# A two-layer transformer on one core: feed-forward weights prepared inside the first projection

## The chip, the cores and the metric

The kernel runs on one core of a Trainium2 chip. The metric is the device time of one execution in microseconds, as the median of several runs. Times in the profile are microseconds from the start of the profiled execution's span, unless they are marked ns. The engines are PE (matrix multiply, with PEld for its weight loads), VectorE (DVE in the profile), ACT, POOL and SP; SP issues the DMAs.

## The reference, cut to what matters

The sequence has 4096 tokens of 256 features in float32. The first layer is an attention with a low-rank key and value path, then a feed-forward part whose operands are rounded to a 4-bit grid in blocks of 16; the second layer is another attention and another feed-forward part.

```python
x = _layernorm(x + _L0_attn_ref(x, W_q, W_dkv, W_uk, W_uv, W_o, ln_gamma, ln_beta))
x = _layernorm(x + _L0_ffn_ref(x, w_gate, w_up, w_down))
x = _layernorm(x + _L1_attn_ref(x, wq, wk, wv, wo_w, wo_b))
x = _layernorm(x + _L1_ffn_ref(x, ...))

def fp4_linear(x, w):            # in _L0_ffn_ref
    xq = fp4_quant_dequant(x)    # blocks of 16 along the last dimension
    wq = fp4_quant_dequant(w)
    return jnp.einsum('bsk,nk->bsn', xq, wq)
gate = fp4_linear(x, w_gate)     # w_gate, w_up: 704 x 256
y = fp4_linear(x, w_up)
h = jax.nn.silu(gate) * y
return fp4_linear(h, w_down)     # w_down: 256 x 704
```

In the first attention, q is rotated by position; a latent of 64 features is made from x, normed, and k and v are made from it; the mask is causal.

## The kernel before

The program is a row of stages with a barrier and a clearing of semaphores between two (`core.clear()`): `project` for layer 0, `attention`, `mlp_weights`, `mlp`, then `project` and `attention` for layer 1, `mix_out` and `coupling`. Within a stage each engine has its own instruction list in program order, and semaphores tie the lists together.

`project` for layer 0 goes through the tokens in eight turns of 512. PE transposes the next turn's x and the rotation tables through a ring of two PSUM banks (`ring`, `turn`), makes the latent (line 358) and q (line 329); VectorE takes the latent's statistics (507, 510, 512), multiplies q by the tables (483, once ahead of the norm and once behind it), norms the latent (519), later multiplies k (483), and forms the remainders of k and q (490). POOL widens the tables (450), takes the root for the norm (471) and adds up the rotations of q and k (459, 460). ACT empties the ring (392, 397, 401), casts the rotated q and k to a high part (408) and keeps v (431). SP, in its own order, stores the high part of k of the turn before, then issues the x and table loads of the next turn (232, 240), then stores q, the remainder of k, v and the remainder of q. So the loads of a turn stand behind the cast and the store of k from the turn before, and POOL's root for a turn stands behind the widening of the next turn's table. In the last turn nothing is loaded any more.

`mlp_weights` loads the three weights (1042, 1044), rounds gate, up and down one after the other on VectorE with the ten steps of `quantize` (989 to 1016, each waiting for the one before), and turns them on PE (1075) into PSUM, from where ACT copies them into `wguT` and `wdT` (1082). `mlp` begins with a load of the output weights and of x (1128, 1132), transposes the attention's output (1143) and mixes it.

Of the kernel before, what the change touches and what calls it, by code (L numbers as in the profile page):

```python
# [27 lines left out]
T = 4096  # L28
# [116 lines left out]

TB = 4
# [3 lines left out]
def project(nc, core, ps, ident, layer, x_dram, x_all, w, tables, q_parts, k_parts, v_dram, ones_to=None):  # L150
# [5 lines left out]
    with ExitStack() as ctx:  # L156
# [6 lines left out]
        if L0:  # L163
            ones = sb("ones", [PARTS, 2048])
# [45 lines left out]


        turns = [("x", 0, 0), ("x", 1, 0), ("t", 0, 0), ("t", 1, 0)]
# [12 lines left out]
        with nc.Block() as block:  # L225
            @block.sync
            def _(sp):
# [43 lines left out]
                if L0:  # L271
                    sp.wait_ge(ones_set, 1)
                    for b in range(2):
                        rows = ones_to[b * HALF + SROWS:b * HALF + MROWS].bitcast(F32).rearrange("p g j t -> p (g j t)")
                        sp.dma_start(rows.rearrange("p (r n) -> p r n", n=2048),
                                     ones[:].unsqueeze(1).to_broadcast([PARTS, 4 * T // 2048, 2048])).then_inc(ones_in, 16)
# [21 lines left out]
            def _(pe):  # L298
# [47 lines left out]

                pe.wait_ge(w_in, 16 * (6 if L0 else 3))
# [3 lines left out]
                for i in range(NB):  # L351
# [27 lines left out]
                    tokens_v(i)  # L379

            @block.scalar
            def _(act):
                def keep(what):
# [9 lines left out]
                    elif kind == "t":  # L393
# [3 lines left out]
                        act.activation(tabT[:, j % 2, m, :], src, ACT.Copy).then_inc(kept, 1)  # L397
                    else:
# [15 lines left out]
                for i in range(NB):  # L414
# [10 lines left out]
                    for g in range(0, TB, 2):  # L425
# [3 lines left out]
                        if i >= 2 and g == 0:  # L429
# [3 lines left out]
                                       ).then_inc(v_kept, 1)  # L433
                cast("k", NB - 1)
# [41 lines left out]
            def _(dve):  # L476
# [16 lines left out]
                if L0:  # L493
                    dve.wait_ge(w_in, 16 * 6)
                    for c in range(DC):
# [3 lines left out]
                                    w_uk[:].rearrange("p (h a d) -> p a h d", a=2, d=half)).then_inc(w_set, 1)  # L499
                for i in range(NB):  # L500
                    if L0:
# [11 lines left out]
                        steps.end()  # L513
                        angle("q", 0, i)
# [15 lines left out]
                    leave("q", i)  # L530
                leave("k", NB - 1)
# [428 lines left out]

QUANT_STEPS = 10


class Quantized:


    def __init__(self, steps, src, dst, n, bufs):
        self.steps, self.src, self.dst = steps, src, dst  # L970
        self.amax, self.scale, self.inv, self.norm, self.step = bufs
        self.p, self.nb = src.shape[0], n // 16

    def blocks(self, ap):
        return ap.rearrange("p (b e) -> p b e", e=16)

    def wide(self, ap):
        return ap.unsqueeze(2).to_broadcast([self.p, self.nb, 16])


def quantize(dve, *lanes):

    for q in lanes:
        q.steps.ready()
        q.steps.put(dve.tensor_reduce(q.amax, q.blocks(q.src), AX.X, ALU.max, apply_absolute_value=True))
    for q in lanes:  # L990
        q.steps.ready()
        q.steps.put(dve.tensor_scalar(q.scale, q.amax, 1.0 / 6.0, 1e-12, ALU.mult, ALU.max))
    for q in lanes:
        q.steps.ready()
        q.steps.put(dve.reciprocal(q.inv, q.scale))
    for q in lanes:
        q.steps.ready()
        q.steps.put(dve.tensor_scalar(q.inv, q.inv, 1.0 - 2.0 ** -22, None, ALU.mult))
    for q in lanes:
        q.steps.ready()  # L1000
        q.steps.put(dve.tensor_tensor(q.blocks(q.norm), q.blocks(q.src), q.wide(q.inv), ALU.mult))
    for q in lanes:
        q.steps.ready()
        q.steps.put(dve.tensor_scalar(q.step.bitcast(U32), q.norm.bitcast(U32), 0x7F800000, None, ALU.bitwise_and))
    for q in lanes:
        q.steps.ready()
        q.steps.put(dve.tensor_scalar(q.step, q.step, 1.0, ROUND, ALU.max, ALU.mult))
    for q in lanes:
        q.steps.ready()
        q.steps.put(dve.tensor_tensor(q.norm, q.norm, q.step, ALU.add))  # L1010
    for q in lanes:
        q.steps.ready()
        q.steps.put(dve.tensor_tensor(q.norm, q.norm, q.step, ALU.subtract))
    for q in lanes:
        q.steps.ready()
        q.steps.put(dve.tensor_tensor(q.blocks(q.dst), q.blocks(q.norm), q.wide(q.scale), ALU.mult))


def quant_bufs(sb, name, p, n):
    return [sb(f"{name}_{x}", [p, n // 16])[:] for x in ("amax", "scale", "inv")] + \  # L1020
           [sb(f"{name}_{x}", [p, n])[:] for x in ("norm", "step")]


def mlp_weights(nc, core, ps, ident, w, wguT, wdT):

    R = 88
    A = FF // R
    with ExitStack() as ctx:
        sb = lambda name, shape, dt=F32: sbuf(nc, ctx, "mw_" + name, shape, dt)
        gu = sb("gu", [R, 2, A * D])  # L1030
        dn = sb("dn", [P, DC * FF])
        gub = quant_bufs(sb, "gub", R, A * D)
        dnb = quant_bufs(sb, "dnb", P, DC * FF)
        w_in = core.sem("mw_in")
        steps_done = core.sem("mw_steps")
        turned = core.sem("mw_turned")
# [769 lines left out]
```

## Time and profile before

| what | us |
|---|---|
| median of three runs | 5320.7 (5313.73 to 5340.69) |
| span of the profiled execution | 5307.5 |
| PE busy in the span | 4955.1 (93%) |
| VectorE busy | 4498.3 (85%) |
| ACT busy | 3777.1 (71%) |
| POOL busy | 315.1 (6%) |

The busy shares are means over stages that differ much: the two attentions fill most of the span. The profiled execution's span runs from its first to its last instruction; the times of the runs hold what lies around it too.

### The profile page before, as it was taken

The numbers are of one execution on the slowest core, as the hardware profiler recorded it, in microseconds if no ns is written. First come the engines' busy times: TensorE is split into PE (matmuls) and PEld (weight loads), VectorE is DVE, ScalarE is ACT, GpSimd is POOL, SyncE is SP. The second block draws the span as 40 slices with busy tenths as digits, with TensorE's granted clock in tenths as the row PEclk, the third lists the DMA queues.
The fourth block names the chain that finished last, engine by engine and source line by source line (L and its number), as shares of the span: only waits on it lengthen the run. The fifth ranks groups of instructions, "written<-read, shape, count | busy, mean of one in ns | idle before, by whom it ended". The sixth has DMA issues, their size and how long they took to land. (4 is left out here: it accounts for less than half of the span.)

```text
span 5307.5 us, 101793 instructions
## 1 busy us (share of the span) xinstructions
PE 4955.1 (93%) x42036; PEld 2017.7 (38%) x42036; DVE 4498.3 (85%) x5080; ACT 3777.1 (71%) x7189; POOL 315.1 (6%) x482
## 2 busy tenths in 40 slices
PE   7699999999999588877999999999999999999998
PEld 4333433433333245542333333333333333333343
DVE  3688889889886579849999999999999999999346
ACT  2177778787787422232888888888888888888853
POOL 3200000000000011130000000000000000000030
PEclk7589999999998789996999999999999999999999
DMA  4301010010000000051100001000010000000000
GB/s 131 107 23 28 11 29 21 14 40 11 11 8 7 21 17 13 10 196 39 43 5 8 5 4 43 8 5 5 11 37 8 5 5 8 8 4 5 9 1 32
DMA packets 138202, 131.30 MB, mean 25 GB/s; under 512 B 61803, under 2 KB 96491, under 8 KB 137707
## 3 DMA queue, kind: packets, MB, share of 16 engines
q1 hardware_dynamic: 137738, 124.80, 8.3%
q8 instruction: 331, 5.42, 0.4%
q14 instruction: 133, 1.08, 0.1%
HBM read 76.75 MB, written 46.66 MB: 23 GB/s over the span
## 5 line engine op out<-in xcount | busy, mean ns | idle before, releaser
L915 DVE TENSOR_REDUCE att_mx<-ps 128x2 f32<-128x1024 f32 (+2 forms) x3200 | 3746.5, 1192 | 263.1 <-PE ps L801 185.1
L898 ACT ACTIVATE att_probs<-ps 128x512 f32<-128x512 f32 (+3 forms) x6400 | 3385.5, 583 | 596.3 <-PE ps L839 284.5
L864 PE MATMUL ps<-att_probs,att_V 128*17 128x256 f32 (+1 forms) x25088 | 1958.6, 387 | 0.3
L839 PE MATMUL ps<-att_Q,K 50*128 50x512 f32 (+3 forms) x6400 | 1686.9, 492 | 43.9 <-ACT att_probs L898 21.0
L801 PE MATMUL ps<-K,att_Q 48*128 48x512 f32 (+2 forms) x6400 | 1397.3, 414 | 91.7 <-DVE att_mx L915 54.7
L839 PEld LDWEIGHTS ps<-att_Q,K 50*128 50x128 f32 x6400 | 657.0, 185 | 1395.2 <-ACT att_probs L898 1269.7
L864 PEld LDWEIGHTS ps<-att_probs,att_V 128*17 128x17 f32 x25088 | 425.5, 95 | 1065.1 <-issue 597.3
L801 PEld LDWEIGHTS ps<-K,att_Q 48*128 48x128 f32 x6400 | 651.1, 192 | 173.6 <-DVE att_mx L915 122.1
L726 POOL TENSOR_SCALAR_AFFINE_SELECT att_probs<-att_probs 128x512 f32<-128x512 f32 x128 | 81.2, 635 | 1512.8 <-ACT att_probs L898 1512.8
L1169 PE MATMUL ps<-wguT,mlp_xqT 128*128 128x512 f32 (+1 forms) x384 | 159.7, 566 | 0.6 <-DVE mlp_h L1277 0.2
L1368 POOL MEMSET mix_power<- 128x1 f32 x1 | 0.1, 98 | 2655.1 <-POOLq L131 2655.1
L879 ACT ACTIVATE att_negT<-ps 32x128 fp32r<-32x128 f32 x64 | 16.2, 253 | 184.6 <-PE ps L811 184.6
L952 DVE RECIPROCAL att_rden<-att_out 128x16 f32<-128x16 f32 x64 | 16.3, 254 | 148.3 <-ACT att_out L903 148.3
L1208 ACT ACTIVATE mlp_gate<-ps 128x704 f32<-128x704 f32 x32 | 24.2, 757 | 139.9 <-PE ps L1169 139.9
L483 DVE TENSOR_TENSOR proj_qprod<-ps,proj_tabT 128x1024 f32<-128x1024 f32 x32 | 38.4, 1220 | 80.2 <-PE ps L329 80.2
L1169 PEld LDWEIGHTS ps<-wguT,mlp_xqT 128*128 128x128 f32 x384 | 72.0, 194 | 72.8 <-issue 64.4
L1187 PE MATMUL ps<-wdT,mlp_hqT 128*128 128x256 f32 (+1 forms) x384 | 95.5, 391 | 1.1 <-DVE mlp_y L1256 1.1
L1607 PE MATMUL ps<-xT_all,net_w 128*128 128x512 f32 x192 | 95.1, 618 | 0.0
L392 ACT ACTIVATE proj_xT<-ps 128x512 f32<-128x512 f32 x32 | 17.5, 595 | 107.3 <-PE ps L311 107.3
L1555 DVE TENSOR_SCALAR cn_cf<-cn_th,cn_ab 128x512 f32<-128x512 f32 x24 | 13.1, 546 | 83.5 <-ACT cn_th L1689 83.0
L1187 PEld LDWEIGHTS ps<-wdT,mlp_hqT 128*128 128x128 f32 (+1 forms) x384 | 70.8, 191 | 27.0 <-issue 12.4
L791 PE MATMUL ps<-att_band,att_pick 64*128 64x128 bf16 x1024 | 79.8, 225 | 0.0
(207 smaller groups left out, 2383.1 us busy)
## 6 DMA issues: line engine op xcount, KB each, us to landing
att_Q<-qhi_scratch SPq DMA_DIRECT2D x256, 64.0 KB, 2.3
K<-khi_scratch SPq DMA_DIRECT2D x256, 64.0 KB, 2.3
v_scratch<-proj_vpad SPq DMA_DIRECT2D x16, 544.0 KB, 3.4
att_V<-v_scratch SPq DMA_DIRECT2D x64, 136.0 KB, 2.5
att_Q<-qlo_scratch SPq DMA_DIRECT2D x128, 64.0 KB, 2.3
K<-klo_scratch SPq DMA_DIRECT2D x128, 64.0 KB, 2.4
proj_x<-in_L_attn_x SPq DMA_DIRECT2D x8, 512.0 KB, 5.4
qhi_scratch<-proj_qhipart SPq DMA_DIRECT2D x16, 256.0 KB, 3.0
```

The lines of the kernel that those rows point to most:

```text
L483: dve.tensor_tensor(prod[name][:, m], of[name], tabT[:, j % 2, m, :].unsqueeze(1).to_broadcast([P, 2, B]), ALU.mult).then_inc(prods[name], 1)
L726: pool.affine_select(out=square, in_=square, compare_op=ALU.is_ge, fill=0.0, base=0, pattern=[[0, GH], [1, P]], channel_multiplier=-1).the ...
L791: return pe.matmul(dst, pick[rows, m], band[rows, m], start=False, stop=(m == 1))
L801: mm = pe.matmul(bank(b)[:, 0:wide], Q[rows, slot_of(u), j, qt * P:(qt + 1) * P], K[rows, par_of(u), j, c * QB:c * QB + wide], start=True, ...
L839: mm = pe.matmul(ring(at)[:, lo:QB], K[rows, par_of(u), j, kt * P:(kt + 1) * P], Q[rows, slot_of(u), j, lo:QB], start=True, stop=True)
L864: mm = pe.matmul(ps[VW * h:VW * h + HV, 6, lo:(part + 1) * (QB // 2)], V[:, par_of(v), kt, HV * h:HV * (h + 1)], probs[:, (n_key[v] + kt) ...
L898: act.activation(probs[:, (n_key[u] + kt) % PBUFS, column(h), lo:QB], ring(at)[:, lo:QB], ACT.Exp, scale=SCALE).then_inc(emptied, 1)
L915: dve.tensor_reduce(mx[:, min(u % NQB, 1), :, j, qt, c], ps[:, 2 + 2 * pair:4 + 2 * pair, 0:max_width(u, i) // 2], AX.X, ALU.max).then_inc ...
L1169: mm = pe.matmul(gu_ps[:, b:to], xqT[:, par, c, :], wguT[:, c, b:to], start=(c == 0), stop=(c == DC - 1))
L1187: mm = pe.matmul(down, hqT[0:kw, par, k, :], wdT[0:kw, k, :], start=(k == 0), stop=(k == NK - 1))
L1208: act.activation(gate[:], gate_ps, ACT.Silu).then_inc(s["gate_kept"], 1)
L1607: mm = pe.matmul(bank1(k, m), nets.w1[:, c, m * P:(m + 1) * P], xT_all[:, c, cols_of(k)], start=(c == 0), stop=(c == DC - 1))
```

## The change

The stage `mlp_weights` is taken out. The three weights are loaded in layer 0's `project` by SP, behind the second turn's loads, into `a_all`, which attention fills only later; `a_all` also holds the rounding's work space. They are rounded on VectorE in ten pieces, four each of gate and up (88 x 512) and two of down (128 x 704), two in each of the turns 1 to 5: one behind the latent's statistics, one at the end of the turn. In turns 6 and 7 PE turns them in seven groups each at the end of the turn, through the same ring, and ACT copies them out. `wguT` and `wdT` are allocated around the projection and attention. The tile of ones is half as wide, and its copies into K have twice as many rows.

```diff
+class Rounding:
...
+    def loads(self):
+        out = [(self.gu[:, i].rearrange("p (a d) -> p a d", a=WA), self.w[name].rearrange("(a p) d -> p a d", p=WR))
+               for i, name in enumerate(("w_gate", "w_up"))]
+        return out + [(self.dn.rearrange("p (a k) -> p a k", a=DC), self.w["w_down"].rearrange("(a p) k -> p a k", p=P))]
+    def piece(self, steps, n):
+        i, n = ROUNDED[n]
+        part = self.gu[:, i, n * WCOLS:(n + 1) * WCOLS] if i < 2 else self.dn[:, n * FF:(n + 1) * FF]
...
-            ones = sb("ones", [PARTS, 2048])
+            ones = sb("ones", [PARTS, 1024])
...
+                if i in W_TURNS:
+                    turns += [("w", n, i) for n in W_TURNS[i]]
...
                 load(1)
                 if L0:
+                    for dst, src in rounding.loads():
+                        sp.dma_start(dst, src).then_inc(mlp_in, 16)
                     sp.wait_ge(ones_set, 1)
...
+                def turn_weights(i):
+                    for n in W_TURNS.get(i, ()):
+                        pe.wait_ge(mlp_steps, len(ROUNDED) * QUANT_STEPS)
+                        dst = ring(number["w", n, i])
+                        for m, (src, rows, cols) in enumerate(rounding.turns[n][1]):
+                            mm = pe.transpose(dst[0:cols, m * rows:(m + 1) * rows], src, ident[0:rows, 0:rows])
+                        mm.then_inc(turned, 1)
...
                     tokens_v(i)
+                    if L0:
+                        turn_weights(i)
...
+                    elif kind == "w":
+                        dst, items = rounding.turns[m]
+                        act.activation(dst, src[0:dst.shape[0], 0:len(items) * items[0][1]], ACT.Copy).then_inc(kept, 1)
...
+                    if L0:
+                        for n in W_TURNS.get(i, ()):
+                            keep(("w", n, i))
                 cast("k", NB - 1)
...
+                def round_piece(n):
+                    if 0 <= n < len(ROUNDED):
+                        if n == 0:
+                            dve.wait_ge(mlp_in, 48)
+                        steps = Chain(dve, mlp_steps, n, QUANT_STEPS)
+                        quantize(dve, rounding.piece(steps, n))
+                        steps.end()
...
                         steps.end()
+                        round_piece(2 * (i - 1))
                         angle("q", 0, i)
...
                     leave("q", i)
+                    if L0:
+                        round_piece(2 * (i - 1) + 1)
```

`W_TURNS` is {6: range(7), 7: range(7, 14)}; the first eight groups are gate and up, the last six down.

## Rows read from the trace of the kernel before

**Rows 1.** Busy us by stretch: length; PE, PEld, DVE, ACT, POOL; PEclk, DMA share, GB/s

```profile
0.00:198.00 198.00, 143.12 (x448) 86.85 (x448) 74.62 (x155) 51.09 (x73) 73.48 (x66) 0.74 0.46 134
...
1800.40:1862.20 61.80, 8.98 (x44) 6.50 (x44) 41.57 (x30) 6.00 (x14) 0.00 (x0) 0.50 0.15 35
...
99.10:121.06 21.96, 17.41 (x57) 10.57 (x56) 9.25 (x19) 6.14 (x9) 9.07 (x8) 0.73 0.46 132
```

**Rows 2.** Timeline at the weight stage's ends: start us, length us, engine, line, operation

```profile
1799.94 0.43 DVE L956 TENSOR_TENSOR a_all<-att_out,att_rden 128x256 f32<-128x256 f32 x1
1801.24 0.32 SPq L1042 DMA_DIRECT2D mw_gu<-in_L_ffn_w_gate  x1
...
1862.20 0.39 SPq L1128 DMA_DIRECT2D mlp_wo<-in_L_attn_W_o  x1
```

**Rows 3.** Timeline: first and last rounding steps on VectorE, gate and down

```profile
1814.93 2.28 DVE L989 TENSOR_REDUCE mw_gub_amax<-mw_gu 88x128 f32<-88x2048 f32 x1 [14.56 <-DMA mw_dn<-in_L_ffn_w_down]
...
1828.22 2.29 DVE L1016 TENSOR_TENSOR mw_gu<-mw_gub_norm,mw_gub_scale 88x2048 f32<-88x2048 f32 x1
...
1846.16 1.62 DVE L989 TENSOR_REDUCE mw_dnb_amax<-mw_dn 128x88 f32<-128x1408 f32 x1
...
1855.87 1.62 DVE L1016 TENSOR_TENSOR mw_dn<-mw_dnb_norm,mw_dnb_scale 128x1408 f32<-128x1408 f32 x1
```

**Rows 4.** Timeline of one turn of the projection's loop; last, the norms by tile

```profile
97.02 1.22 DVE L490 TENSOR_TENSOR proj_qlopart<-proj_qrot,proj_qhipart 128x1024 fp32r<-128x1024 f32 x1
...
97.18 2.17 POOL L459 TENSOR_TENSOR proj_krot<-proj_kprod 128x512 f32<-128x512 f32 x1 [2.60 <-DVE proj_kprod L483]
...
99.32 1.26 POOL L460 TENSOR_TENSOR proj_krot<-proj_kprod 128x512 f32<-128x512 f32 x1
...
101.82 1.58 SPq L248 DMA_DIRECT2D khi_scratch<-proj_khipart  x2
...
102.82 0.62 DVE L507 BATCH_NORM_STATS2 proj_st<-ps 128x6 f32<-128x64 f32 x4 [4.58 <-PE ps L358]
...
103.89 0.17 DVE L512 TENSOR_SCALAR proj_var<-proj_mv 128x4 f32<-128x4 f32 x1
...
107.88 1.23 DVE L483 TENSOR_TENSOR proj_qprod<-ps,proj_tabT 128x1024 f32<-128x1024 f32 x1 [3.82 <-PE ps L329]
...
109.55 1.16 POOL L450 COPY proj_wide<-proj_tab 128x512 f32<-128x512 f32 x2 [8.97 <-DMA proj_tab<-in_sin]
...
110.68 1.02 POOL L471 TENSOR_TENSOR proj_rstd<-proj_var,proj_power 128x4 f32<-128x4 f32 x1
...
111.73 1.10 DVE L519 TENSOR_SCALAR proj_lat<-ps,proj_mv,proj_rstd 128x64 f32<-128x64 f32 x4 [2.63 <-POOL proj_rstd L471]
...
L519 DVE TENSOR_SCALAR proj_lat<-ps,proj_mv,proj_rstd x32: 333/338/347, 23.9 to 178.3; 128x64 f32<-128x64 f32 x32
```

**Rows 5.** Timeline in the second layer's projection: a product on VectorE, a rotation on POOL

```profile
2312.20 2.36 DVE L483 TENSOR_TENSOR proj_kprod<-ps,proj_tabT 128x1024 f32<-128x1024 f32 x2
...
2313.35 1.26 POOL L460 TENSOR_TENSOR proj_qrot<-proj_qprod 128x512 f32<-128x512 f32 x1
```

**Rows 6.** Timeline in the weight stage: transposes of gate (four groups) and of down (six)

```profile
1830.57 2.90 PE L1075 MATMUL ps<-ident,mw_gu 88*128 88x88 f32 x16 [31.58 <-DVE mw_gu L1016]
...
1857.55 3.57 PE L1075 MATMUL ps<-ident,mw_dn 128*128 128x128 f32 x12 [8.47 <-DVE mw_dn L1016]
```

**Rows 7.** Timeline of the last turn of the first projection

```profile
171.28 5.05 PE L329 MATMUL ps<-proj_xT,proj_wqp 128*128 128x512 f32 x8
...
187.71 0.60 ACT L431 ACTIVATE proj_vpad<-ps 128x512 f32<-128x512 f32 x1 [2.16 <-PE ps L339]
...
189.11 1.06 ACT L408 ACTIVATE proj_khipart<-proj_krot 128x1024 fp32r<-128x1024 f32 x1 [0.80 <-POOL proj_krot L460]
```

**Rows 8.** Timeline of SP's queue: the copies of ones, the first store of q

```profile
8.72 1.54 SPq L275 DMA_DIRECT2D K<-proj_ones  x2
...
29.82 1.24 SPq L248 DMA_DIRECT2D qhi_scratch<-proj_qhipart  x2
```

More of the change, by code:

```diff
@@ L143, in tok, with __init__, blocks, wide @@
     return bass.ds(j * n, n)
+QUANT_STEPS = 10
+class Quantized:
+    def __init__(self, steps, src, dst, n, bufs):
+        self.steps, self.src, self.dst = steps, src, dst
+        self.amax, self.scale, self.inv, self.norm, self.step = bufs
+        self.p, self.nb = src.shape[0], n // 16
+    def blocks(self, ap):
+        return ap.rearrange("p (b e) -> p b e", e=16)
+    def wide(self, ap):
+        return ap.unsqueeze(2).to_broadcast([self.p, self.nb, 16])
+def quantize(dve, *lanes):
+    for q in lanes:
+        q.steps.ready()
+        q.steps.put(dve.tensor_reduce(q.amax, q.blocks(q.src), AX.X, ALU.max, apply_absolute_value=True))
+    for q in lanes:
+        q.steps.ready()
+        q.steps.put(dve.tensor_scalar(q.scale, q.amax, 1.0 / 6.0, 1e-12, ALU.mult, ALU.max))
+    for q in lanes:
+        q.steps.ready()
+        q.steps.put(dve.reciprocal(q.inv, q.scale))
+    for q in lanes:
+        q.steps.ready()
+        q.steps.put(dve.tensor_scalar(q.inv, q.inv, 1.0 - 2.0 ** -22, None, ALU.mult))
+    for q in lanes:
+        q.steps.ready()
+        q.steps.put(dve.tensor_tensor(q.blocks(q.norm), q.blocks(q.src), q.wide(q.inv), ALU.mult))
+    for q in lanes:
+        q.steps.ready()
+        q.steps.put(dve.tensor_scalar(q.step.bitcast(U32), q.norm.bitcast(U32), 0x7F800000, None, ALU.bitwise_and))
+    for q in lanes:
+        q.steps.ready()
+        q.steps.put(dve.tensor_scalar(q.step, q.step, 1.0, ROUND, ALU.max, ALU.mult))
+    for q in lanes:
+        q.steps.ready()
+        q.steps.put(dve.tensor_tensor(q.norm, q.norm, q.step, ALU.add))
+    for q in lanes:
+        q.steps.ready()
+        q.steps.put(dve.tensor_tensor(q.norm, q.norm, q.step, ALU.subtract))
+    for q in lanes:
+        q.steps.ready()
+        q.steps.put(dve.tensor_tensor(q.blocks(q.dst), q.blocks(q.norm), q.wide(q.scale), ALU.mult))
@@ L274, in _ @@
                         rows = ones_to[b * HALF + SROWS:b * HALF + MROWS].bitcast(F32).rearrange("p g j t -> p (g j t)")
-                        sp.dma_start(rows.rearrange("p (r n) -> p r n", n=2048),
-                                     ones[:].unsqueeze(1).to_broadcast([PARTS, 4 * T // 2048, 2048])).then_inc(ones_in, 16)
+                        sp.dma_start(rows.rearrange("p (r n) -> p r n", n=1024),
+                                     ones[:].unsqueeze(1).to_broadcast([PARTS, 4 * T // 1024, 1024])).then_inc(ones_in, 16)
                 for i in range(NB + 1):
@@ L959, in _ @@
                                 ALU.mult).then_inc(out_read, 1)
[L963 to L978, printed above, removed]
@@ L981, in quantize @@
[L981 to L1016, printed above, removed]
@@ L1743, in build @@
             wdT = sbuf(nc, own, "wdT", [P, -(-FF // P), D])
[L1744 to L1745 removed]
+            m = {"w": {"w_gate": t["L0_ffn_w_gate"], "w_up": t["L0_ffn_w_up"], "w_down": t["L0_ffn_w_down"]},
+                 "guT": wguT, "dT": wdT, "space": a_all}
+            project(nc, core, ps, ident, 0, x0, None, w0, (t["cos0"], t["sin0"]), q_parts, k_parts, v_dram, K, m)
+            core.clear()
+            attention(nc, core, ps, ident, 0, True, q_parts, k_parts, v_dram, K, a_all)
             core.clear()
```

96 lines of the change are left out of this document (33 added, 63 removed).

## The prediction

> **What bounds the kernel now.** I read the busy times by stage first, then the timeline at the seam between the first attention and the feed-forward stage, then the timeline of one turn of the first projection's loop, last the instructions that share a resource with what is moved in. The reader is to see three things.
>
> First, the weight stage is a piece of the span in which one engine after the other works alone. In its 61.8 us VectorE is busy 41.57 us, ACT 6.00, PE 8.98, POOL 0.00 [rows 1]. The last result of attention starts at 1799.94 us, the stage's first load is issued at 1801.24, the next stage's first load at 1862.20 [rows 2]. Up to 1814.93 it waits for its loads, then VectorE rounds without a break until 1857.49 (1855.87 + 1.62) [rows 3], then the last transposes run [rows 6]. Nothing of another stage lies beside it: all of it is on the path.
>
> Second, the projection has room on VectorE: 74.62 us busy of 198, and 9.25 in a turn of 21.96 us [rows 1].
>
> Third, this room is not on the loop that sets the turn's length. In the turn shown, POOL rotates k (97.18 and 99.32), ACT casts it, SP stores it at 101.82 and only then issues the next x and table loads; POOL widens the table when it has landed (109.55), takes the root, and VectorE norms the latent at 111.73, from which the next k is made [rows 4]. From the end of the q remainder (97.02 + 1.22 = 98.24) to the norm at 111.73 VectorE has 13.49 us and works in two spells: the statistics, 102.82 to 104.06, and one product of 1.23 at 107.88 [rows 4]. The rest, 13.49 - 1.24 - 1.23 = 11.02 us, is idle. The norms of the eight turns (32 instructions) run from 23.9 to 178.3 us, so a turn is about 22 us [rows 4].
>
> **What goes.** The stage with its barrier, first load to first load of the next: 1862.20 - 1801.24 = 60.96 us [rows 2]. The feed-forward stage's start is otherwise the same chain, beginning with the load of the output weights. PE comes to it from attention and not from a stage with a granted clock of 0.50 [rows 1]; that may save up to 2 us (estimate) while its pipeline fills. I take 0.
>
> **The loads.** Three DMA issues move to SP, behind the second x and table load and ahead of the copies of ones. From first issue to landing they took 13.7 us [rows 2, 3]. They take the place of the copies of ones at 8.72, so they land near 23; SP has nothing else to issue before the q store at 29.82 [rows 8], and VectorE asks for them only in turn 1, later still. Queued behind them are the copies of ones, halved in size per descriptor and needed only at the end of the stage. Cost 0; if the q store came into them, at most the 13.7.
>
> **The pieces on VectorE.** The chain of ten instructions took 15.58 us on 2048 columns (1814.93 to 1830.51) and 11.33 on 1408 (1846.16 to 1857.49) [rows 3]: 6.63 ns a column. That gives 11.33 - 896 x 0.00663 = 5.39 us for a piece of 512 and 6.66 for one of 704 columns, in all 8 x 5.39 + 2 x 6.66 = 56.4 us. Turns 1 to 5 take two each: one behind the statistics, one behind the q remainder. Behind the first wait the product and the norm, behind the second the next turn's statistics.
>
> So each of the four gaps between turns 1 and 5 gets 10.78 us (the last 12.05, with the first piece of 704) into a room of 11.02. Without anything else it just fits: the statistics slip from 102.82 to 103.6, which nobody needs before the root; the product ends near 111.6. The ninth and tenth pieces are halves of other gaps: turn 1's first lies in the loads' wait of its own turn, turn 5's second delays statistics whose root has to wait for a load anyway.
>
> But POOL works in this gap too. Where VectorE reads two SBUF operands (the q remainder, 97.02, 1.22 us), the POOL rotation beside it takes 2.17 us, against 1.26 for its twin [rows 4]; it made no progress until 98.24. Beside a product with one operand in PSUM (2312.20 to 2314.56) the same rotation takes 1.26 [rows 5]. So the four two-operand steps of a piece and POOL's instructions exclude each other, and VectorE, nearly full, pays for that. Bounds for one gap, from POOL's rows: 0, and all that POOL does in it: 1.11 + 1.26 of rotation, 1.16 of widening (109.55) and 1.02 of root (110.68), 4.55 us [rows 4]. I take the first part of the rotation's 1.2 (it runs beside the first steps of a piece in every turn) and half the widening's 1.16 (it meets only the last steps): 1.8, less the 0.15 us of room left: 1.65. Four gaps: 6.6, the longer piece 1.3: 8 us. Bounds 1.3 and 4 x 4.55 + 1.3 = 20.
>
> The Trainium skill, SBUF — State Buffer, section "Who interferes with whom", says that the shared port pair is held for a whole instruction by whoever starts first, and that fast fp32 tensor_scalar steps take it too, while tensor_reduce never does. The trace agrees on the two-operand steps (2.17 against 1.26); of the tensor_scalar steps no row shows it. By that rule the small scale step would wait out the rotation's first half, some 0.3 us a turn, and the sum would be 1 us worse (estimate).
>
> **The transposes.** In the removed stage 16 transposes of gate or up weights (four groups) took 2.90 us, 0.73 a group, and twelve of the down weights (six groups) 3.57, 0.60 a group, at the low clock [rows 6]. Turn 6 gets seven groups of the first kind, 5.1 us of PE time ahead of turn 7's latent matmuls. Turn 7 has no load to wait for, so PE leads it and this is on the path. Part comes back: turn 7's q matmuls take 5.05 us [rows 7], and PE goes into them warmer; at a turn's granted clock of 0.73 [rows 1] they would take 5.05 x 0.73 = 3.7 if the clock were full from the first one (estimate). I take 5.1 - 1.4 = 3.7, bounds 2 (the latent matmuls too) and 5.1. The wait for all ten pieces is over before: the last one starts two turns of 22 us behind 98.24 and takes 6.66, so it ends near 149, near 160 with every slip counted below; the transposes come at about 168. ACT's seven copies stand ahead of the k cast of turn 6, which no load waits for any more.
>
> Turn 7 gets one group of the first kind and six of the second, 0.73 + 6 x 0.60 = 4.3 us, plus a last copy of some 0.5, between its last v copy and its k cast. They start when that v copy does, at 187.71, and end at 192.5; the cast stood at 189.11 [rows 7], so the cast, the remainder and the last store slip by 3.4 us, bounds 2.5 and 3.9 (a group more or less). ACT runs in order, so the cast can't pass the copies.
>
> **Sum.** 8 + 3.7 + 3.4 = 15 us given back (bounds 1.3 + 2 + 2.5 = 6 and 20 + 5.1 + 3.9 = 29), of 61: 46 us gained, between 32 and 55 (57 with the warm start). Profiled, 5307.5 becomes 5261.5. That span is 6.2 us under the fastest and 13.2 under the median of the three runs, 5320.7; I take the difference off the median: 5275.
>
> **Rivals.**
> (a) The room is enough: POOL slips between the steps and nothing is paid but the transposes and the long piece. For it: the loop hangs on a load, and POOL is idle most of the turn. Against it: 0.2 us of spare in 11. 5321 - 55 = 5266.
> (b) POOL starves: the steps of a chain follow each other at once (ten in 11.33 us, their gaps included) [rows 3], and the rotation's second half, which is on the loop, gets the port only when the piece is over, near 98.28 + 5.39, and ends at 104.9 instead of 100.6: 4.35 us in four turns and 5.6 in the fifth, 23. With the loads later the first pieces then have room. 61 - 23 - 7 = 31: 5290. Against it: the rotation's second half starts while VectorE is at its first, one-operand step or soon behind it.
> (c) Slower: the pieces find no cover at all, because POOL and VectorE take turns through all of both, and the loop becomes their sum. 56.4 + 5 x 4.55 + 7 = 86, against 61: 25 us slower, 5346. It decides from the point where the pieces put over 54 us (61 - 7), 96% of their length, on the path. Against it: between the end of the k store's issue (101.82 + 1.58) and the widening at 109.55 the loop needs neither engine for 6 us [rows 4].
> (d) The loads don't hide: the q store, or the second x load, comes behind them, up to 13.7 us: 5288.
>
> **Chances.** Forecast 0.61, (a) 0.20, (b) 0.12, (c) 0.03, (d) 0.04. Range: from (a) with the warm start and the spread of the runs (7 us under the median) at 5258, to 5296 past (b) and (d). About 0.5% (26.6 us, below 5294) is what a measurement of this kernel can tell from no change: forecast and (a) lie below it, (b) and (d) near it. Faster 0.86, same 0.11, slower 0.03.
>
> **What would show it.** The profile after: feed-forward's first load about 1 us behind attention's last result; projection ending near 213 instead of 198; two chains of some 5.4 us in turns 1 to 5; turns of 23 to 25 us there. The statistics late but the norm hardly: (a). A rotation of 4 us or more: (b). The turn 7 latent matmuls 5 us behind turn 6's v. Wrong would be: attention or feed-forward of another length, since I count on neither changing; or a gap that grows by more than 4.6 us.

## The result and the profile after

The changed kernel took 5267.2 us (median; 5264.1 to 5268.3), the kernel before, on the same chip, 5326.6 (5313.7 to 5340.7): a ratio of 0.9883 with an interval of 0.9856 to 0.9910, 59 us less. Two later comparisons of the same pair gave 0.9891 and 0.9909. The forecast was 46 us less, 5275 with a range of 5258 to 5296.

The profiled execution's span is 5264.5 us, against 5307.5 before. Line numbers from here on are those of the kernel that each row comes from. First the windows of the projection, of one turn (from the latent's matmuls to the next turn's, as in [rows 1]), and of the first attention (length; PE, PEld, DVE, ACT, POOL; PEclk, DMA share, GB/s):

```profile
0.00:214.20 214.20, 157.67 (x492) 95.54 (x492) 131.26 (x256) 57.09 (x87) 77.15 (x66) 0.71 0.46 134
102.49:125.84 23.35, 18.17 (x57) 10.84 (x57) 20.14 (x40) 6.26 (x9) 9.84 (x8) 0.72 0.41 122
214.20:1822.30 1608.10, 1529.93 (x14496) 611.48 (x14496) 1310.89 (x1313) 1193.34 (x2400) 83.76 (x138) 0.93 0.07 20
```

VectorE, busy 9.25 us of a turn of 21.96 before [rows 1], is busy 20.14 us of 23.35. The projection ends at 214.2 instead of 198.1. The seam, on the timeline:

```profile
1822.32 0.42 DVE L1092 TENSOR_TENSOR a_all<-att_out,att_rden 128x256 f32<-128x256 f32 x1
1823.62 0.40 SPq L1141 DMA_DIRECT2D mlp_wo<-in_L_attn_W_o  x1
```

From attention's last result to feed-forward's first load it is 1.3 us instead of 62.3 [rows 2]. Stage by stage, the two profiled executions differ by: seam -61.0, projection +16.1, first attention +6.3 (1608.1 against 1601.8), feed-forward and second projection +1.0, second attention -5.4, the rest 0.0. The sum is -43.0, the difference of the spans.

The start of the projection, on SP's queue and at the first piece:

```profile
8.72 0.51 SPq L380 DMA_DIRECT2D a_all<-in_L_ffn_w_gate  x1
...
11.01 1.73 SPq L380 DMA_DIRECT2D a_all<-in_L_ffn_w_down  x1
12.78 1.52 SPq L384 DMA_DIRECT2D K<-proj_ones  x2
29.87 1.24 SPq L355 DMA_DIRECT2D qhi_scratch<-proj_qhipart  x2
...
36.84 0.17 DVE L645 TENSOR_SCALAR proj_var<-proj_mv 128x4 f32<-128x4 f32 x1
36.91 0.68 DVE L172 TENSOR_REDUCE proj_round_amax<-a_all 88x32 f32<-88x512 f32 x1
```

The loads cost nothing: the first q store stands at 29.87, where it was at 29.82 [rows 8], and the first piece (line 172) starts directly behind the statistics (line 645), with no wait for its weights.

One turn with both its pieces, the counterpart of [rows 4] (start us, length us, engine, line, operation; in brackets the engine's idle time before and what ended it):

```profile
100.41 1.22 DVE L615 TENSOR_TENSOR proj_qlopart<-proj_qrot,proj_qhipart 128x1024 fp32r<-128x1024 f32 x1
...
100.57 2.18 POOL L584 TENSOR_TENSOR proj_krot<-proj_kprod 128x512 f32<-128x512 f32 x1 [3.63 <-DVE proj_kprod L608]
101.54 0.67 DVE L172 TENSOR_REDUCE proj_round_amax<-a_all 88x32 f32<-88x512 f32 x1
102.25 0.54 DVE L175 TENSOR_SCALAR proj_round_scale<-proj_round_amax 88x32 f32<-88x32 f32 x1
...
102.71 1.27 POOL L585 TENSOR_TENSOR proj_krot<-proj_kprod 128x512 f32<-128x512 f32 x1
...
103.20 0.82 DVE L181 TENSOR_SCALAR proj_round_inv<-proj_round_inv 88x32 f32<-88x32 f32 x1
...
107.74 0.61 DVE L640 BATCH_NORM_STATS2 proj_st<-ps 128x6 f32<-128x64 f32 x4
...
108.88 0.67 DVE L172 TENSOR_REDUCE proj_round_amax<-a_all 88x32 f32<-88x512 f32 x1
109.59 0.18 DVE L175 TENSOR_SCALAR proj_round_scale<-proj_round_amax 88x32 f32<-88x32 f32 x1
...
112.87 2.06 POOL L575 COPY proj_wide<-proj_tab 128x512 f32<-128x512 f32 x2 [8.90 <-DMA proj_tab<-in_sin]
...
113.48 0.98 DVE L199 TENSOR_TENSOR a_all<-a_all,proj_round_scale 88x512 f32<-88x512 f32 x1
114.38 1.21 DVE L608 TENSOR_TENSOR proj_qprod<-ps,proj_tabT 128x1024 f32<-128x1024 f32 x1
...
114.90 1.01 POOL L596 TENSOR_TENSOR proj_rstd<-proj_var,proj_power 128x4 f32<-128x4 f32 x1
...
115.95 1.10 DVE L653 TENSOR_SCALAR proj_lat<-ps,proj_mv,proj_rstd 128x64 f32<-128x64 f32 x4 [0.35 <-POOL proj_rstd L596]
```

POOL's rotation is as long as before (2.18 and 1.27, against 2.17 and 1.26). It was VectorE that waited there: its 32-column steps took 0.54 and 0.82 us beside the rotation, 0.18 away from it (109.59). At the other end both waited: the widening took 2.06 us beside the second piece's last two steps, 1.16 before, and the last step took 0.98. Root and norm follow it, so from the end of the q remainder (101.63) to the norm it is 14.32 us; it was 13.49.

The last turn, with the transposes of turn 6 ahead of it:

```profile
174.85 5.25 PE L461 MATMUL ps<-ident,a_all 88*128 88x88 f32 x28
...
179.89 3.58 PE L475 MATMUL ps<-proj_wlat,proj_xT 128*128 128x64 f32 x16
...
183.26 5.93 PE L438 MATMUL ps<-proj_xT,proj_wqp 128*128 128x512 f32 x8
...
190.36 1.09 DVE L653 TENSOR_SCALAR proj_lat<-ps,proj_mv,proj_rstd 128x64 f32<-128x64 f32 x4
...
203.10 3.06 PE L461 MATMUL ps<-ident,a_all 128*128 128x128 f32 x10 [0.22 <-ACT wguT L519]
...
206.48 1.04 ACT L530 ACTIVATE proj_khipart<-proj_krot 128x1024 fp32r<-128x1024 f32 x1
...
208.81 1.19 SPq L355 DMA_DIRECT2D klo_scratch<-proj_klopart  x2
```

### The profile page after: what moved, and what is told of

Same layout as the page of the kernel before. It is cut to its first block and busy times, and to the rows that moved or that the text cites. A ratio compares the mean times of both kernels' runs of the same rounds, so it can differ in the third digit from the quotient of the medians.

```text
span 5264.5 us, 101841 instructions
## 1 busy us (share of the span) xinstructions
PE 4963.0 (94%) x42036; PEld 2022.6 (38%) x42036; DVE 4507.2 (86%) x5150; ACT 3776.7 (72%) x7189; POOL 318.8 (6%) x482
## 5 line engine op out<-in xcount | busy, mean ns | idle before, releaser
L975 PE MATMUL ps<-att_Q,K 50*128 50x512 f32 (+3 forms) x6400 | 1689.7, 493 | 42.7 <-ACT att_probs L1034 21.7
L1015 ACT ACTIVATE att_negT<-ps 32x128 fp32r<-32x128 f32 x64 | 16.1, 252 | 183.4 <-PE ps L947 183.4
L1182 PEld LDWEIGHTS ps<-wguT,mlp_xqT 128*128 128x128 f32 x384 | 72.1, 195 | 73.4 <-issue 65.0
```

Of the source, the lines that this page charges most:

```text
L975: mm = pe.matmul(ring(at)[:, lo:QB], K[rows, par_of(u), j, kt * P:(kt + 1) * P], Q[rows, slot_of(u), j, lo:QB], start=True, stop=True)
L1182: mm = pe.matmul(gu_ps[:, b:to], xqT[:, par, c, :], wguT[:, c, b:to], start=(c == 0), stop=(c == DC - 1))
```

## Experiments

The theory: the stage's 61 us go off the path, and some 15 come back, from three places: two-operand steps of the pieces that meet POOL, transposes ahead of the last turn, and transposes ahead of its last cast of k. The rivals: the time moved with the addresses of the weights or the granted clock of the first attention; the removed stage was not worth its length; VectorE's fullness, not the meeting with POOL, stretches the turns.

### How much two executions of one kernel differ: the same two kernels again

`changed_again` and `changed_third` are the changed kernel, `before_look1` and `before_look2` the kernel before, all unedited.

> The changed kernel once more, against the kernel before on the same chip. Open is why the runs moved by 62 us (5326.57 to 5267.22) where the two spans moved by 43 (5307.5 to 5264.5) and the stages, each measured from its first instruction to the next stage's, by 43 too. Theory A: the change is worth the 44 us that the stages show (61 less 16 for the projection, with the two attentions 6 us up and 5 down by chance), and the kernel before drew two long runs; then this call's ratio lies near 0.992 and the first attention is anywhere from 1600 to 1609 us long. Theory B: the change is worth over 55 us in most executions, because the kernel before is often longer in a stage that its one profile does not show long; then the ratio stays at 0.988 to 0.990 and the spans of the kernel before scatter by 20 us while those of the changed one stay within 5.

> The changed kernel a third time. Open is still whether it gains the 48 us that the mean stage lengths of the profiles give (62.5 - 1.3 for the removed stage, 13.4 for the projection: 212.4 as the mean of two profiles against 199.0 of five) or more. The first attention scatters from 1592 to 1648 us with a granted clock of 0.94 to 0.90, in kernels with the weight stage and without, and nothing else does. Theory A: ratio 0.989 to 0.993 and a first attention within that scatter. Theory B (the change also shortens the first attention): ratio 0.985 to 0.988.

> The kernel before, unchanged, for a second profile. Its first profile (span 5307.5, granted clock 0.948) is shorter than 17 of 17 later executions, whose spans lie between 5318.4 and 5352.4 at a clock of 0.946 to 0.938. Theory A (the gain is the 44 us that the stages show, the rest is which executions were drawn): a profile of usual length is longer in the two attentions by 20 to 30 us together and by under 3 us in every other stage; then a changed kernel's usual profile has attentions of the same length. Theory B (something of the change makes the attentions shorter): the attentions of the kernel before are usually 10 us or more above the 1605 to 1617 and 2640 to 2651 us of the four profiles of changed kernels.

> The same once more; the two profiles show how far the stages of one kernel scatter. Expected as for the first: projection 197 to 199 us, the weight stage with its barriers 62 to 63, the stretch from the feed-forward part to the second attention 522 to 525, the last stages 277; all scatter above 3 us in the two attentions.

Measured: ratios of 0.9891 (0.9867 to 0.9914) and 0.9909 (0.9888 to 0.9931); spans of 5281.3 and 5280.7 for the changed kernel, 5321.9 and 5356.5 for the one before. The projection took 210.6 and 212.6 us with the change, 202.1 and 198.9 without it. The first attention took 1617.4 and 1620.9 with it, 1605.4 and 1647.9 without. The windows of the first attention in the kernel before (its first and its third profile):

```profile
198.10:1799.90 1601.80, 1522.91 (x14496) 608.89 (x14496) 1310.90 (x1313) 1192.92 (x2400) 83.75 (x138) 0.94 0.08 20
```

```profile
198.90:1846.80 1647.90, 1571.52 (x14496) 623.29 (x14496) 1313.81 (x1313) 1193.81 (x2400) 84.16 (x138) 0.90 0.08 20
```

The same 14496 matmuls of the same code: 46 us apart, at a mean granted clock of 0.94 and 0.90. What follows: two spans alone can't carry a claim of some 10 us; the lengths of the projection, which scatter by 4.4 us with the stage and by 3.6 without, and of the seam can. The ratio of 0.9891 lies where the second theory of the first repeat put it, but the changed kernel's executions scatter by 22 us (5268 to 5290), not within 5; the 0.9909 lies in the first theory's range. The times don't decide between the two. Nor was the second profile of the kernel before as expected: its 14 us over the first lie in the projection (4), both attentions (4 each) and the feed-forward part (3), and not in the attentions alone.

### The addresses alone

```diff
-            ones = sb("ones", [PARTS, 2048])
+            ones = sb("ones", [PARTS, 1024])
...
-        project(nc, core, ps, ident, 0, x0, None, w0, (t["cos0"], t["sin0"]), q_parts, k_parts, v_dram, K)
...
+            project(nc, core, ps, ident, 0, x0, None, w0, (t["cos0"], t["sin0"]), q_parts, k_parts, v_dram, K)
```

The kernel before, with `wguT` and `wdT` allocated around the projection and attention and the tile of ones halved.

> The kernel before with its weight stage kept, but with the two tensors of turned weights allocated around the projection and the first attention, and the tile of ones halved, as in the changed kernel: the same addresses without the moved work. The first attention took 1601.9 us before and 1608.2 in the changed kernel. If the addresses do that, this kernel's first attention is near 1608 and the time 6 us above the kernel before. If it is chance of the granted clock, attention stays anywhere within 1600 to 1609 and the time is that of the kernel before within 0.2%.

Measured: 0.9975 (0.9956 to 0.9995); projection 197.7, seam 62.5.

```profile
197.70:1790.10 1592.40, 1513.24 (x14496) 606.12 (x14496) 1310.00 (x1313) 1192.39 (x2400) 83.77 (x138) 0.94 0.08 20
```

The new places don't lengthen attention. The ratio is 13 us of 5335 below one, and in the profile only the first attention is shorter, by less than the kernel before differs from itself. Whether that is a gain of the addresses stays open.

### What one such stage is worth

```diff
+            mlp_weights(nc, core, ps, ident, {"w_gate": t["L0_ffn_w_gate"], "w_up": t["L0_ffn_w_up"],
+                                              "w_down": t["L0_ffn_w_down"]}, wguT, wdT, "mv_")
+            core.clear()
```

> The kernel before with its weight stage run a second time (the same loads, rounding and transposes into the same tensors). It prices the removed stage by itself: 61 us by the seam of the profile, with nothing moved into the projection. Theory A: the time rises by 61 us, ratio near 1.0115, and the attentions keep their lengths. Theory B: if a stretch in which PE is idle also makes the next stage longer or shorter (through the granted clock), the rise differs from 61 by more than 5 us, and the feed-forward stage's or second attention's length shows it.

Measured: 5385.5 us, 1.0110 (1.0075 to 1.0145), 55 us more than before. That is over 5 us off the 61, the second theory's condition, but the interval reaches from 40 to 77 us, so the time decides nothing; the profile does. The first loads of the two stages and of feed-forward:

```profile
1808.88 0.32 SPq L1042 DMA_DIRECT2D mv_gu<-in_L_ffn_w_gate  x1
...
1870.25 0.30 SPq L1042 DMA_DIRECT2D mw_gu<-in_L_ffn_w_gate  x1
...
1930.89 0.39 SPq L1128 DMA_DIRECT2D mlp_wo<-in_L_attn_W_o  x1
```

61.4 and 60.6 us each. The stages around them stay near their lengths: feed-forward and second projection take 526.1 us, against 522.5 to 525.3 in three profiles of the kernel before. The first term of the sum holds.

### Steps that don't meet POOL

```diff
-                        quantize(dve, rounding.piece(steps, n))
+                        q = rounding.piece(steps, n)
+                        full = q.nb
+                        for nb in (full, 2, full * 14 // 32, 2, full, full * 17 // 32, full * 17 // 32, full, full, full):
+                            steps.ready()
+                            steps.put(dve.tensor_reduce(q.amax[:, 0:nb], q.blocks(q.src)[:, 0:nb], AX.X, ALU.max))
```

The ten steps of a piece become ten reductions with one operand each, of the length that a piece has away from POOL.

> The steps of a piece are replaced by reductions of the same lengths (5.3 us a piece) that read one operand and write only the block maxima; the weights stay unrounded. Theory of the port: in the changed kernel the widening on POOL took 2.0 us in turns 3 to 5 instead of 1.16 and the small scale steps up to 0.82 instead of 0.18, because two-operand and fast steps exclude POOL; here the widening is 1.16 again, no step is stretched, and the gap from the q remainder's end to the norm falls from 14.3 (15.5 in turn 5) to 13.4 to 13.9 us, 2 to 4 us in all. Rival: VectorE is simply full; then the gaps stay at 14.3 and the widening's length does not matter.

Measured: 5266.7 us, 0.9867 (0.9842 to 0.9893); projection 206.9. The same turn, and behind it the second piece of the next, the long one:

```profile
100.17 5.33 DVE L634 TENSOR_REDUCE proj_round_amax<-a_all 88x32 f32<-88x512 f32 x10
...
106.55 5.33 DVE L634 TENSOR_REDUCE proj_round_amax<-a_all 88x32 f32<-88x512 f32 x10
111.80 1.21 DVE L608 TENSOR_TENSOR proj_qprod<-ps,proj_tabT 128x1024 f32<-128x1024 f32 x1
113.19 1.16 POOL L575 COPY proj_wide<-proj_tab 128x512 f32<-128x512 f32 x2 [10.58 <-DMA proj_tab<-in_sin]
114.31 1.02 POOL L596 TENSOR_TENSOR proj_rstd<-proj_var,proj_power 128x4 f32<-128x4 f32 x1
...
130.25 6.66 DVE L634 TENSOR_REDUCE proj_round_amax<-a_all 128x44 f32<-128x704 f32 x10
...
135.47 1.17 POOL L575 COPY proj_wide<-proj_tab 128x512 f32<-128x512 f32 x2 [9.17 <-DMA proj_tab<-in_sin]
```

The widening is back at 1.16 or 1.17 us in every turn. In the turn shown that says little, since the reductions end at 111.88, ahead of the widening; only the long piece (130.25 to 136.91) meets it, and there it takes 1.17. The reductions beside the rotation are no longer than those away from it (5.33 us for either piece). The gaps from the q remainder of turns 1 to 5 to the next norm are 13.97, 14.02, 15.1 (a table that landed late), 14.0 and 13.28, together 70.4 us against 72.1 in the changed kernel and 68.7 with the stage: 1.7 us won, less than the 2 to 4 expected. In the gap shown VectorE works 12.2 us and waits 2.35 for the root; in the changed kernel it works 13.4 and waits 0.35, and the 1.2 between them are about what its steps lose beside POOL (1.0 and 0.29, below). So the meeting with POOL stretches the ordinary turns. In the turn of the long piece VectorE waits for nothing ahead of the norm even here, so there its own work is the bound.

### The transposes without the pieces

```diff
-                        pe.wait_ge(mlp_steps, len(ROUNDED) * QUANT_STEPS)
+                        pe.wait_ge(mlp_in, 48)
...
-                    if 0 <= n < len(ROUNDED):
+                    if False:
```

> The changed kernel without the ten pieces: loads and transposes stay where they are, PE waits for the loads instead of the last piece, and the weights stay unrounded. Theory: turns 1 to 6 are those of the kernel before (gaps of 13.3 to 14.3 us, set by the loads, the widening 1.16), the transposes alone make the stretch between the norms of turns 6 and 7 26 instead of 20 and the k cast of the last turn 3.4 us later, and attention starts at 206.5 to 209.5 against 197.7 to 202.1. Rival: the slower k matmuls and turn 7's unchanged clock in the changed kernel come from the pieces' delay and not from chance or the transposes; then the stretch from norm 6 to norm 7 is below 24 here.

Measured: 5286.6 us in one time; projection 206.9, attention 1627.8 at a granted clock of 0.92. The gaps behind turns 1 to 5 are 13.47, 14.14, 14.76, 13.76 and 13.47, the widening 1.16. From the norm of turn 6 to that of turn 7 it is 24.34 us, from there to the last k cast 14.61 (199.21 - 184.60). With the transposes alone, then, the last turn is as late as in the changed kernel, and the turns before have their old length.

### The transposes where PE waits anyway

```diff
-W_TURNS = {6: range(7), 7: range(7, 14)}
+W_TURNS = {3: range(0, 2), 4: range(2, 4), 5: range(4, 6), 6: range(6, 10), 7: range(10, 14)}
+W_NEED = [4] * 4 + [8] * 4 + [10] * 6
...
-                        pe.wait_ge(mlp_steps, len(ROUNDED) * QUANT_STEPS)
+                        pe.wait_ge(mlp_steps, W_NEED[n] * QUANT_STEPS)
```

The groups are spread over turns 3 to 7 and stand behind the q matmuls, where PE waits for the next load or norm, and no longer behind v; ACT's copies and the ring's order move along.

> The fourteen groups of transposes are taken from the ends of turns 6 and 7 and put behind the q matmuls, where PE waits for the next x to land: two each in turns 3, 4 and 5, four in turn 6, the last four in turn 7 where PE waits for the norm. Theory: the groups at the turns' ends are on the path and cost 5.9 us between the norms of turns 6 and 7 and 3.4 at the end; here they lie under waits, the first attention starts at 205 to 207 us instead of 214.1, and the time falls by 7 to 9 us against the changed kernel. Rival: the projection is held by VectorE and the loads all the same, or the groups push the x transposes back by as much; then attention starts at 212 to 215 and the time is that of the changed kernel.

Measured: 5270.1 us, 0.9883 (0.9851 to 0.9916), beside 0.9891 for the changed kernel in the same comparison: no difference that the times show. The profile shows one: the projection ends at 202.2 (210.6), the norm of turn 6 to that of turn 7 is 18.99 us, and the last k cast stands at 193.38. The transposes themselves are faster too. Two groups, right behind the q matmuls of turn 5:

```profile
132.55:133.32 0.77, 0.77 (x9) 0.60 (x7) 0.77 (x1) 0.26 (x1) 0.00 (x0) 1.00 1.02 244
```

The granted clock is 1.00 there (2.4 GHz), and a group takes 0.39 us; in the changed kernel seven groups took 5.25 at 0.50 (1.2 GHz), 0.75 each.

### The product out of the gap

```diff
-                        angle("q", 0, i)
...
+                        angle("q", 0, i)
```

On top of the last edit, the product of q moves behind the norm, so that VectorE is done sooner.

> The transposes under PE's waits as in the run with the spread transposes, and besides VectorE's first q product goes behind the norm instead of ahead of it. In the changed kernel the gap from the q remainder's end to the norm is 14.31 us in four turns (15.5 with the long piece): VectorE's own work plus what POOL's rotation and widening hold up. Theory: with the product out of the gap it loses up to 1.2 us of work, the loop falls back on the loads and the gap to 13.3 to 14.0; the first attention starts 2 to 4 us earlier than with the spread transposes alone (202.2), at 198 to 200.5, which is what the projection took without any of the moved work. Rival: the gap is set by the widening that the piece holds up (2.0 us instead of 1.16) and by the root behind it; then it stays at 14.0 to 14.3 and attention starts at 201 to 203.

Measured: 5258.9 us, 0.9874 (0.9851 to 0.9897), a projection of 205.6 us, longer than with the spread alone. Two norms in the timeline:

```profile
93.57 1.10 DVE L653 TENSOR_SCALAR proj_lat<-ps,proj_mv,proj_rstd 128x64 f32<-128x64 f32 x4 [2.04 <-POOL proj_rstd L597]
...
116.97 1.10 DVE L653 TENSOR_SCALAR proj_lat<-ps,proj_mv,proj_rstd 128x64 f32<-128x64 f32 x4 [2.04 <-POOL proj_rstd L597]
```

VectorE now idles 1.49 or 2.04 us for POOL's root, with gaps of 13.7 to 15.1, together 71.6 us against 72.1 in the changed kernel, and the product it put off lengthens the other half of the turn. Neither theory had the projection this long. It says what the ordinary gap is: load, widening (which the last steps of a piece hold up), root, norm. The product is not its bound.

### The root ahead of the widening

```diff
-                        if i + 1 < NB:
-                            widen(i + 1)
...
+                        if i + 1 < NB:
+                            widen(i + 1)
```

On top of the spread, POOL takes the root of a turn first and widens the next table behind it.

> The spread transposes, with POOL's root for the norm put ahead of the widening of the next table instead of behind it (and VectorE's product where the changed kernel has it). In the run with the product moved VectorE waited 2.04 us before each norm for the root, which stood behind a widening of 1.6 to 1.7. Theory: the norm then waits for VectorE's own work alone, the gap falls from 14.3 to 13.4 to 13.9, but PE turns the widened tables ahead of the latent, so the latent's transposes wait for the widening as before and the turn wins at most 0.5 us; attention starts between 199 and 203. Rival: the held-up widening and root are the loop; then the turns fall to 22 us and attention starts at 196 to 199.

Measured: 5263.5 us, 0.9886 (0.9858 to 0.9914), beside 5282.3 and 0.9909 for the changed kernel in the same comparison. The same turn:

```profile
107.73 1.02 POOL L595 TENSOR_TENSOR proj_rstd<-proj_var,proj_power 128x4 f32<-128x4 f32 x1 [5.08 <-DVE proj_var L646]
...
111.55 2.07 POOL L576 COPY proj_wide<-proj_tab 128x512 f32<-128x512 f32 x2 [2.80 <-DMA proj_tab<-in_sin]
...
112.16 0.98 DVE L199 TENSOR_TENSOR a_all<-a_all,proj_round_scale 88x512 f32<-88x512 f32 x1
113.06 1.21 DVE L609 TENSOR_TENSOR proj_qprod<-ps,proj_tabT 128x1024 f32<-128x1024 f32 x1
114.20 1.08 DVE L654 TENSOR_SCALAR proj_lat<-ps,proj_mv,proj_rstd 128x64 f32<-128x64 f32 x4
```

Now the norm waits for nobody: VectorE goes straight from the product into it, and the widening's 2.07 us lie beside. Of all the runs with the rounding, only here is VectorE's own work the bound of the gap in an ordinary turn. The projection takes 198.8 us, as long as without any of the moved work (199.2, below). That doesn't show that the pieces are covered. The gaps behind turns 1 to 4, which hold two pieces each, are 14.18, 13.88, 13.90 and 15.50 us, at most 0.7 shorter than with the spread alone (14.34, 14.33, 14.61 and 15.50) and still 2.2 longer together than with the stage. The gain lies where one piece or none stands: behind turns 0, 5 and 6 the gaps fall from 12.17, 13.49 and 10.70 to 10.38, 11.63 and 7.44. This order might shorten the kernel before as well; that was not run. It has the shortest projection of the changed kernels; the two ratios' intervals overlap, so the times don't separate it from the changed kernel.

## Why the prediction was right, point by point

Four profiled executions with the stage (three of the kernel before and that with the addresses alone) and three of the changed kernel give these means, cut at the norms, the q remainders and the last k cast. The kernel with the stage twice, which is not in the means, has 69.8, 43.4, 20.1, 11.4, 8.9 and 198.4.

| part of the projection, us | with the stage | changed | difference | forecast |
|---|---|---|---|---|
| gaps, q remainder of turns 1 to 5 to the next norm, sum | 68.7 | 72.1 | +3.4 | +8 |
| the other halves, norm to q remainder, turns 1 to 5, sum | 45.4 | 48.5 | +3.1 | 0 |
| norm of turn 6 to norm of turn 7 | 19.7 | 24.4 | +4.7 | +3.7 |
| norm of turn 7 to last k cast | 11.9 | 15.3 | +3.4 | +3.4 |
| last k cast to the stage's end | 8.9 | 7.7 | -1.1 | 0 |
| whole projection | 199.2 | 212.5 | +13.2 | +15 |

- **The stage, 60.96 us.** Right: 61.0 in the first pair of profiles, 61.4 and 60.6 when it was added once more. Rivals by which it would not be gained fall with it. Feed-forward's first load came 1.3 us behind attention. The up to 2 us that I thought a warmer start might save did not show: feed-forward and second projection took 522.2 to 524.3 us with the change and 522.5 to 525.3 in the kernel before.
- **The loads, 0.** Right; rival (d) is refuted by the q store at 29.87 and, for the second x load, by the norm of turn 1, at 44.4 to 44.6 us with the change and 44.2 to 45.1 with the stage.
- **The pieces, 8 us.** The mechanism was right, the term too large (3.4 by the means). I had counted a delay of the rotation's first part beside the widening's. But the rotation's first half meets the q remainder with or without a piece (2.17 and 2.18), and beside the piece it was VectorE that waited: its steps lost 1.0 us beside the rotation (0.36 + 0.64) and 0.29 beside the widening, and VectorE was left 0.35 idle. The spare room that the sum took off a gap should have been 0.24 us (11.02 - 10.78), not 0.15. What reaches the norm is the widening. Two neighbouring turns of `changed_third` show how:

```profile
90.49 1.63 POOL L575 COPY proj_wide<-proj_tab 128x512 f32<-128x512 f32 x2 [9.34 <-DMA proj_tab<-in_sin]
90.65 0.99 DVE L199 TENSOR_TENSOR a_all<-a_all,proj_round_scale 88x512 f32<-88x512 f32 x1
...
114.02 1.17 POOL L575 COPY proj_wide<-proj_tab 128x512 f32<-128x512 f32 x2 [10.38 <-DMA proj_tab<-in_sin]
```

  Behind the end of the q remainder, the widening starts at 11.25 us in the turn shown first and takes 2.06; here it starts at 11.69 and takes 1.63. Both end at 13.3, 0.5 behind the piece's last step: the end of the piece sets it, and the gap is 14.3 either way. Where the table lands behind the piece (12.73, the second turn) the widening takes 1.17 and the load sets the gap, 14.92. So the 1.0 us that the steps lose beside the rotation is not free, since it pushes the last steps into the widening. Half of the 3.4 comes from the gap with the long piece: 15.5 us in all three executions, 1.65 more than with the stage, and there VectorE goes into the norm without a wait, so it is full. Rival (b) needed a rotation of 4 us or more, and its second half was 1.27 long and began 2.14 behind the first, as before.
- **The scale step.** The scale step beside the rotation took 0.54 instead of 0.18 us, 0.36 more, where I had worked out 0.3. This agrees with the Trainium skill, SBUF — State Buffer, section "Who interferes with whom": steps of this kind can take the shared pair too, while `tensor_reduce` never contends. The 1.17 of the widening beside the long piece's reductions shows the second half. The extra 1 us that I drew from it for the sum can't be read off as a term of its own: all that the pieces cost in the gaps is 3.4.
- **Transposes ahead of turn 7, 3.7 us.** Near in size (4.7), with one wrong step: the credit of 1.4 us for a warmer PE. The windows of the transposes and of the q matmuls behind them, and of the same q matmuls before:

```profile
174.85:180.10 5.25, 5.07 (x31) 4.35 (x30) 0.00 (x0) 3.38 (x7) 1.48 (x2) 0.50 0.81 258
183.26:189.19 5.93, 5.92 (x9) 2.27 (x9) 1.18 (x9) 0.00 (x0) 1.02 (x1) 0.61 0.21 72
```

```profile
171.28:176.33 5.05, 5.04 (x9) 1.95 (x9) 1.18 (x9) 0.00 (x0) 1.02 (x1) 0.72 0.63 201
```

  The transposes ran at a granted clock of 0.50, the lower level of 1.2 GHz, throughout (0.55 and 0.50 in the other two executions). The q matmuls behind them had 0.61 here, 0.74 and 0.67 in the other two, and took 5.93, 4.94 and 5.46 us; in the four executions with the stage they took 5.02 to 6.07. So the 1.4 us were not gained, and nothing clear of the scatter was lost. From the q remainder of turn 6 to the statistics of turn 7, which leaves the q matmuls out, it is 9.53, 8.61 and 9.65 us instead of 4.58 (once 4.22): 4.8 more in the mean, nearer to the bound of 5.1 without the credit.
- **The end, 3.4 us.** The mean slip of the cast was right to the tenth, which is chance, since from the norm of turn 7 to the cast single executions have 14.6 to 16.1 us with the change and 11.5 to 12.8 with the stage; 1.1 of it came back behind it. The last stores of k went out at 207.55 and 208.81 with nothing of q ahead of them, while before the change the q remainder's store (188.75, 1.57 us long) stood directly ahead of them.
- **The other halves of the turns, 0.** They grew by 3.1. They hold the k matmuls, whose time varies with the granted clock in every kernel (1.98 to 3.78 us for the four of a turn, 8.15 to 10.39 for a half), and the projection's clock was 0.71 with the change and 0.74 before [rows 1]. Whether the change does this is not settled: these sums are 43.4 to 46.8 with the stage and 47.9 to 49.0 in the changed kernel, which speaks for it; but they are 45.6 with the transposes alone, 45.6 with all the pieces and the spread transposes, and 42.7 with the reductions.
- **The rest.** Attention and feed-forward were not to change. By the stages' means the change is worth 61.1 - 13.2 = 48 us; the times say 59, 54 and 42. What lies above 48 in the first comparison is not explained by any stage; the first attention, 1592 to 1648 us in kernels with the stage and 1604 to 1633 without, scatters enough for it. That it gets shorter through the change is neither shown nor excluded, and the addresses alone, 13 us below the kernel before by their ratio, may be part of the gain.
- **The sum.** That the projection's 13 us come so near to the 15 is in part luck: the pieces cost 4.6 us less in the gaps than forecast, the other halves 3.1 more, the transposes ahead of turn 7 1.0 more, and 1.1 came back at the end.
- **Rivals (a) and (c).** (a) left the gaps of the ordinary turns unchanged; behind turns 1 to 3 they grew by 0.3 to 1.0 us, 0.6 in the mean, so it was nearly right there. Its 5266 is nearer to the first median than the forecast, but 13 us came back by the stages' means, nearer to the forecast's 15 than to its 6 (61 - 55). (c) needed 54 us of pieces on the path; 3.4 were.

## What to carry to other kernels

A stage in which engines work one behind the other can give most of its length (here 61 us, less 13) if an earlier stage has an engine that is idle off its loop; look for the chain that sets the loop (here load, widening, root, norm) and put the moved work beside it, not into it. As long as that engine keeps some room, what is charged is not its time but what the moved steps do to others on the chain: two-operand VectorE steps made a POOL copy 0.9 us longer in a turn, of which 0.6 in the mean reached the gap; where the room was gone, with the long piece, the gap grew by 1.65. Moving POOL's root out of that chain shortened the gaps with two pieces by 0.7 us at most, those with one or none by 1.8 to 3.3. Put moved matrix work where PE waits for something else: ahead of the last turn and its cast it cost 7 us (4.7 + 3.4 - 1.1), behind the q matmuls nearly none by the profile, where it also ran at twice the granted clock.

## What was not expected of the hardware

- A 32-column fp32 step of VectorE takes 0.18 us alone and 0.54 or 0.82 beside a POOL tensor-tensor instruction: it ends with that instruction (102.79 and 102.75, 104.02 and 103.98). The two engines take turns instruction by instruction, and neither starved, although VectorE issued ten steps in a row.
- The same attention ran for 1592 to 1648 us at mean granted clocks of 0.94 to 0.90: one code, 46 us of scatter between executions of the kernel before alone.
- 28 transposes in a row, begun behind the v matmuls and their waits, ran at a granted clock of 0.50 to 0.55 in all three executions of the changed kernel; right behind the q matmuls, in groups of eight and more, they had 1.00.
